# Gated cross-attention block with routed experts: the projection of the first query half is moved from the end of a step to between scores and attend

## The chip, the core and the metric
The kernel runs on one core of a Trainium2 chip. The metric is device time in microseconds (us) of one execution. Three runs of the kernel before gave 631.08, 633.39 and 633.51 us; their median is 633.39 us. A profiled execution of the same kernel gives the rows that are quoted below.

## What is computed
There are 64 sequences of 64 tokens with 128 features, so 4096 tokens. The attention part of the reference, cut to what matters here:

```python
q = (emb @ Wq.T)        # emb = layernorm(x); 16 heads of 64
k = (context @ Wk.T)
v = (context @ Wv.T)
q = _layernorm(q, qn_w, qn_b)
k = _layernorm(k, kn_w, kn_b)
attn = jax.nn.softmax(einsum('bhqd,bhkd->bhqk', q, k) * scale)
out = einsum('bhqk,bhkd->bhqd', attn, v)
x = x + tanh(g) * (out @ Wu.T + bu)
```

After it come a second layer norm, a router that picks 2 of 8 experts for each token, the experts' two-layer networks, a shared expert, and a second gated residual. The change touches the attention part only.

## The kernel before, in words
The tokens are cut into 32 tiles of 128 (two sequences each). A software pipeline runs over steps `s` from -5 to 35. Each engine has its own `step(s)` (ACT from L471, POOL from L645, DVE from L897, PE from L1245), which lists in fixed order what that engine does for several tiles at different stages. The order on each engine is written out by hand, and the engines meet at semaphores. An engine runs its list strictly in order, so an instruction that waits holds up all that stands behind it on that engine.

The tile of a step, in the order of its life:
- `project_qk(n, j, t)` (L1063): the projection of queries (n=0) or keys (n=1), first or second half of the heads (j), as three matmuls of 512 columns (high by high part, low by high, high by low; L1059 to L1061) into PSUM bank `2n+j`. It waits for `n_ready[n][j]`, that is until DVE's `scale` has read what the tile before left in that bank.
- `square` on ACT (L372), `sum_squares` on DVE (L747), a short Newton chain on POOL (L598 to L612), `scale` on DVE (L754): the layer norm of queries and keys.
- `transpose_qk` on PE (L1091), then `transposed` on ACT (L396).
- `project_v` on PE, then `values` on ACT (L404).
- `scores(t)` on PE (L1117): 64 matmuls of 64x64. DVE's `maximum` (L762) and `less_maximum_of` (L769) read them, ACT's `exponential` follows (L411), DVE's `row_sums` (L776) and `row_inverses` (L783), and POOL's `normalise_rows` (L618).
- In the next step `transpose_probabilities` on PE (L1100), `probabilities` on ACT (L418), `attend` on PE (L1132, again 64 matmuls of 64x64), `outputs` on ACT (L426), `project_out` on PE (L1147), `residual` on DVE (L730).
- Later: the second layer norm, `logits` (L1171 on PE, read by `keep_logits`, L794 on DVE), the routing chain on DVE (`route`, L840 to L855, from step 11 on in most steps), and POOL's `scatter` of rows to DRAM (two indirect DMAs a step from step 17 on, L636).

In ACT's step the order around the change is: `probabilities` of tile s-1, `log_variance` and `inverse_root` of the keys, `square(0, 0, s + 2)`, `outputs` of tile s-1 (two), `square(0, 1, s + 2)`, `transposed(0, 0, s + 1)`, `transposed(0, 1, s + 1)`, `exponential(s)`. On DVE, `keep_logits(s - 4)` and `route` stand ahead of the next step's `sum_squares(0, ..)`, `scale(1, 0, ..)`, `row_sums` and `row_inverses`, and then comes `residual`, for which PE's last `transpose_qk` of the step waits. On POOL, `normalise_rows` ends a step and `scatter` begins the next.

Of the kernel before, what the change touches and what calls it, by code (L numbers as in the profile page):

```python
# [41 lines left out]
def flamingo_block(nc, x, xT, ctxT, g_xattn, g_ffn, wqT, wkT, wvT, wuT, bu, qn_w, qn_b, kn_w, kn_b,  # L42
                   wg, w1, b1, w2, b2, ws1, bs1, ws2, bs2, out):

    with ExitStack() as stack:
# [186 lines left out]
        def has(t):  # L232
            return 0 <= t < TILES
# [815 lines left out]
        def _(pe):  # L1049
# [8 lines left out]
            def project(out_bank, t, src, w, j):  # L1058
                nc.tensor.matmul(out_bank, xc_hi[:, t % XD, src, :], w_hi[:, w, cols[j]], start=True, stop=False)  # L1059
                nc.tensor.matmul(out_bank, xc_hi[:, t % XD, src, :], w_lo[:, w, cols[j]], start=False, stop=False)  # L1060
                return nc.tensor.matmul(out_bank, xc_lo[:, t % XD, src, :], w_hi[:, w, cols[j]], start=False, stop=True)  # L1061

            def project_qk(n, j, t):  # L1063
                if has(t):
                    if t == 0:
                        pe.wait_ge(w_ready, (3 if n == 0 else 1) + j)
                    pe.wait_ge(xlo_ready, t + 1)
                    if t >= 1:
                        pe.wait_ge(n_ready[n][j], t)
                    project(ps[2 * n + j][:, :], t, n, n, j).then_inc(proj_done[n][j], 1)  # L1070
# [14 lines left out]
            def transpose_qk(n, j, t, bank_free):  # L1085
                if has(t):
                    bank_free(j, t)
                    pe.wait_ge(n_ready[n][j], t + 1)
                    for a in range(4):
                        c0 = (4 * j + a) * P  # L1090
                        last = nc.tensor.transpose(ps[6 + j][:, a * P:(a + 1) * P], qk_n[:, n, c0:c0 + P], ident[:, :])  # L1091
                    last.then_inc(t_done[n][j], 1)

            def transpose_probabilities(j, t, bank_free):
                if has(t):
                    bank_free(j, t)
                    if j == 0:
                        pe.wait_ge(p_ready, t + 1)
                    for a in range(4):
                        last = nc.tensor.transpose(ps[6 + j][:, a * P:(a + 1) * P],  # L1100
                                                   prob[:, 4 * j + a, :, :].rearrange("p b n -> p (b n)"), ident[:, :])
                    last.then_inc(pt_done[j], 1)

            def scores(t):
                if has(t):
                    for j in range(2):
                        pe.wait_ge(v_ready[j], t + 1)
                    for n in range(2):
                        for j in range(2):
                            pe.wait_ge(T_ready[n][j], t + 1)  # L1110
                    for a in range(PAIRS // 2):
                        for b in range(2):
                            for j in range(2):
                                for h in range(2):
                                    rows = slice(h * HD, (h + 1) * HD)
                                    outs = slice((h ^ j) * HD, ((h ^ j) + 1) * HD)
                                    last = nc.tensor.matmul(ps[4 + j][outs, (2 * a + b) * S:(2 * a + b + 1) * S],  # L1117
                                                            qk_T[rows, 0, 2 * a + j, b * S:(b + 1) * S],
                                                            qk_T[rows, 1, 2 * a + j, b * S:(b + 1) * S], start=True, stop=True)
                    last.then_inc(s_done, 1)  # L1120

            def attend(t):
                if has(t):
                    for j in range(2):
                        pe.wait_ge(pt_ready[j], t + 1)
                    for p in range(PAIRS):
                        at = p % 2 * (PAIRS // 2) + p // 2
                        for h in range(2):
                            for b in range(2):
                                rows = slice(b * S, (b + 1) * S)  # L1130
                                q = (h ^ (p % 2)) * S
                                last = nc.tensor.matmul(ps[6 + b][h * HD:(h + 1) * HD, p * S:(p + 1) * S],  # L1132
                                                        v_sb[rows, t % 2, (2 * p + h) * HD:(2 * p + h + 1) * HD],
                                                        prob_T[rows, at, q:q + S], start=True, stop=True)
                                if p == PAIRS - 1 and h == 1:
                                    last.then_inc(o_done[b], 1)
# [25 lines left out]
            def logits(t):  # L1162
                if has(t):
                    if has(t + 4):
                        pe.wait_ge(sub_ready[1], t + 5)
                    else:
                        pe.wait_ge(lg_ready, t)
                    if t == 0:
                        pe.wait_ge(wg_in, 16)
                    pe.wait_ge(rT_ready, t + 1)  # L1170
                    nc.tensor.matmul(ps[5][:, 0:E], row_T[:, t % 2, :], wg_raw[:, :], start=True, stop=True).then_inc(lg_done, 1)  # L1171
# [10 lines left out]
            def route_ranks(s, lag):  # L1182
                b, at = batch_at(s, lag)
                if b is not None and at == RANKS_AT:
                    ranks(b)

            def transpose_tokens(g):
                pe.wait_ge(norm_ready, GT * g + GT)
                if g == 0:
                    pe.wait_ge(sub_ready[0], TILES)  # L1190
                else:
                    pe.wait_ge(f_lo, g)
                for j in range(GT):
                    last = nc.tensor.transpose(ps[4][:, j * P:(j + 1) * P], rows_all[:, GT * g + j, 0:D], ident[:, :])
                last.then_inc(f_t, 1)

            def shared_hidden(g):
                pe.wait_ge(f_lo, g + 1)
                if g == 0:
                    pe.wait_ge(ffw_ready, len(W1_STEPS))  # L1200
                    pe.wait_ge(w2_in, 3 * 16)
                hi, lo = g_parts[:, g % 2, 0, :], g_parts[:, g % 2, 1, :]
                for c in range(CH):
                    fs = slice(c * P, (c + 1) * P)
                    if g > 0:
                        pe.wait_ge(act_ready, CH * (g - 1) + c + 1)
                    nc.tensor.matmul(ps[c][:, :], w1_hi[:, E, fs], hi, start=True, stop=False)
                    nc.tensor.matmul(ps[c][:, :], w1_hi[:, E, fs], lo, start=False, stop=False)
                    nc.tensor.matmul(ps[c][:, :], w1_lo[:, E, fs], hi, start=False, stop=True).then_inc(h_done, 1)
# [35 lines left out]
            def step(s):  # L1245
                if s == TILES:
                    transpose_tokens(0)
                    transpose_tokens(1)
                    shared_hidden(0)
                transpose_probabilities(0, s - 1, before_p)  # L1250
                transpose_probabilities(1, s - 1, before_p)
                scores(s)
                attend(s - 1)
                project_qk(0, 1, s + 2)
                transpose_qk(0, 0, s + 1, before_q)
                logits(s - 4)
                route_ranks(s, ROUTE_LAG)
                transpose_qk(0, 1, s + 1, before_q)
                project_qk(1, 1, s + 2)
                project_v(0, s + 1)  # L1260
                transpose_normed(s - 3)
                project_out(s - 1)
                transpose_qk(1, 0, s + 1, before_k)
                project_qk(1, 0, s + 2)
                transpose_qk(1, 1, s + 1, before_k)
                project_v(1, s + 1)
                project_qk(0, 0, s + 3)
                if s == TILES:
                    transpose_tokens(2)
                if s == TILES + 1:  # L1270
                    shared_hidden(1)
            steps(step)

            shared_result(0)
# [89 lines left out]
```

## Time and profile before
| what | value |
|---|---|
| three runs | 631.08, 633.39, 633.51 us (median 633.39) |
| span of the profiled execution | 671.8 us (the page gives no other total for it) |
| instructions in the trace | 21158 |
| stretch of the attention steps | about 32 to 414 us of the span |
| matmul instructions | 7642 |

How to read it: the profile is of one execution, and its span of 671.8 us is longer than any of the three runs, so its rows are good for durations, orders and waits, and a sum made of them is a difference against the same span. PE is TensorE's matmuls, PEld its weight loads, DVE VectorE, ACT ScalarE, POOL GpSimd. Matmuls are pipelined: the time from the start of one to the start of the next is what a matmul costs the engine, not its own busy time. An idle time "<-issue" is one in which the engine waited for nothing that the profile shows.

### The profile page before, as it was taken

What the parts mean: (1) busy time and instruction counts of PE and PEld (TensorE: products, weight loads), DVE (VectorE), ACT (ScalarE), POOL (GpSimd) and SP (SyncE); (2) the same over time, 40 slices, a digit from 0 to 9 for tenths busy, and PEclk for the clock granted to TensorE, in tenths of its full rate; (3) what the DMA queues carried; (4) which work ended last, traced back from release to release, by engine and by line L of the source; (5) the groups of instructions that cost most, each with busy time, mean ns of one, the idle gap of its engine ahead of it and who ended that gap; (6) DMA issues with size and microseconds to landing.
All of it is one profiled execution on the core that took longest, in us unless ns stands there. A gap on an engine that the chain in (4) does not pass through costs nothing.

```text
span 671.8 us, 21158 instructions
## 1 busy us (share of the span) xinstructions
PE 586.6 (87%) x7642; PEld 517.3 (77%) x7642; DVE 456.0 (68%) x997; ACT 453.3 (67%) x986; POOL 361.4 (54%) x706
## 2 busy tenths in 40 slices
PE   3889999999999999999999987868979988989930
PEld 1578888888888887877887865766979988989930
DVE  4688889898998888887888874464244534444418
ACT  3688899999897887887887863532525444545425
POOL 2545656565666677677677564554105535545530
PEclk9899999999999999999999999978989989999985
DMA  7900100001001001002000000123102212212228
GB/s 242 282 2 3 34 18 29 24 3 49 4 17 43 26 14 47 25 12 64 11 14 16 10 14 21 34 92 100 41 1 77 76 59 71 73 65 77 73 87 316
DMA packets 22583, 38.01 MB, mean 57 GB/s; under 512 B 5233, under 2 KB 13041, under 8 KB 22353
## 3 DMA queue, kind: packets, MB, share of 16 engines
q1 hardware_dynamic: 17648, 27.27, 12.8%
q0 software_dynamic: 4544, 9.38, 3.9%
q8 instruction: 63, 1.03, 0.7%
q14 instruction: 40, 0.32, 0.2%
q10 hardware_dynamic: 288, 0.00, 0.0%
HBM read 23.17 MB, written 13.47 MB: 55 GB/s over the span
## 4 chain that ended last, share of the span: by engine, by line
PE 74%; DVE 8%; issue 7%; DMA 3%; POOL 2%; ACT 2%; another core or an unknown queue 1%; SPq 0%; ACTq 0%; DVEq 0%; POOLq 0%
PE ps L1317 9%; PE ps L1091 7%; PE ps L1147 7%; PE ps L1059 6%; PE ps L1117 6%; PE ps L1061 5%; PE ps L1060 5%; PE ps L1100 4%; PE ps L1219 4%; PE ps L1132 4%; PE ps L1303 3%; PE ps L1305 3%; PE ps L1304 3%; DMA rows_all<-results 1%; DVE wide L754 1%
## 5 line engine op out<-in xcount | busy, mean ns | idle before, releaser
L670 POOL DMA_INDIRECT results<-spo,xs_ix x78 | 75.2, 965 | 100.9 <-DVE spo L1033 85.9
L522 ACT ACTIVATE qk_T<-ps,b_cols 128x256 f32<-128x256 f32 x156 | 61.8, 475 | 75.7 <-PE ps L1305 74.3
L396 ACT ACTIVATE qk_T<-ps,lnw 128x512 f32<-128x512 f32 x128 | 96.8, 787 | 6.0 <-PE ps L1091 5.4
L1059 PE MATMUL ps<-w_hi,xc_hi 128*128 128x512 f32 x192 | 88.3, 460 | 7.9 <-DVE wide L754 3.7
L754 DVE TENSOR_TENSOR wide<-ps,rstd 128x512 f32<-128x512 f32 x128 | 87.2, 681 | 3.9 <-POOL rstd L612 3.9
L747 DVE TENSOR_REDUCE ss<-wide 128x16 f32<-128x1024 f32 x64 | 77.9, 1218 | 15.5 <-ACT wide L372 13.9
L636 POOL DMA_INDIRECT routed<-rows_all,slot x64 | 64.4, 1006 | 29.9 <-issue 16.0
L1091 PE MATMUL ps<-ident,wide 128*128 128x128 f32 x512 | 78.4, 278 | 2.1 <-DVE wide L754 1.0
L372 ACT ACTIVATE wide<-ps 128x512 f32<-128x512 f32 x128 | 76.1, 596 | 3.2 <-PE ps L1061 3.2
L1061 PE MATMUL ps<-w_hi,xc_lo 128*128 128x512 f32 x192 | 77.2, 402 | 0.0
L1317 PE MATMUL ps<-w_sb,qk_T 128*128 x624 | 76.9, 277 | 0.0
L1060 PE MATMUL ps<-w_lo,xc_hi 128*128 128x512 f32 x192 | 76.5, 398 | 0.0
L1317 PEld LDWEIGHTS ps<-w_sb,qk_T 128*128 128x128 f32 x624 | 73.7, 194 | 0.0
L1091 PEld LDWEIGHTS ps<-ident,wide 128*128 128x128 f32 x512 | 59.2, 145 | 18.3 <-ACT spo L426 7.4
L618 POOL TENSOR_TENSOR prob<-prob,rinv 128x1024 f32<-128x1024 f32 x32 | 61.0, 1907 | 14.9 <-DVE rinv L783 14.7
L762 DVE TENSOR_REDUCE mx<-ps 128x8 f32<-128x512 f32 x64 | 41.2, 686 | 34.5 <-PE ps L1117 34.5
L1147 PE MATMUL ps<-wu_sb,spo 128*128 128x128 f32 x512 | 63.8, 279 | 0.1
L1147 PEld LDWEIGHTS ps<-wu_sb,spo 128*128 128x128 f32 x512 | 61.1, 195 | 3.2 <-issue 0.3
L426 ACT ACTIVATE spo<-ps 128x512 f32<-128x512 f32 x64 | 34.8, 596 | 40.8 <-PE ps L1132 40.8
L1303 PE MATMUL ps<-w_lo,w_hi 128*128 128x256 f32 x156 | 48.7, 312 | 9.4 <-DVE w_lo L1003 9.2
L1117 PE MATMUL ps<-qk_T 64*64 64x64 f32 x2048 | 46.0, 223 | 10.5 <-issue 10.4
L1117 PEld LDWEIGHTS ps<-qk_T 64*64 64x64 f32 x2048 | 37.7, 134 | 20.0 <-issue 19.9
(169 smaller groups left out, 1323.4 us busy)
## 6 DMA issues: line engine op xcount, KB each, us to landing
v_sb<-routed SPq DMA_DIRECT2D x39, 130.0 KB
xc_in<-in_x SPq DMA_DIRECT2D x8, 256.0 KB, 2.9
xc_in<-in_ctx SPq DMA_DIRECT2D x8, 256.0 KB, 4.5
w_raw<-in_L_ffn_W SPq DMA_DIRECT2D x8, 256.0 KB, 2.5
wide<-results SPq DMA_DIRECT2D x4, 512.0 KB, 5.1
rows_all<-results SPq DMA_DIRECT2D x4, 512.0 KB, 8.0
out_x<-x_res SPq DMA_DIRECT2D x8, 256.0 KB, 4.1
x_res<-in_x SPq DMA_DIRECT2D x1, 1792.0 KB, 8.5
```

The costliest lines, as they stand in the source:

```text
L372: nc.scalar.activation(sq[:, n, j * 512:j * 512 + 512], ps[2 * n + j][:, :], ACT.Square, scale=HD ** -0.5).then_inc(sq_ready[n][j], 1)
L396: nc.scalar.activation(qk_T[:, n, 4 * j:4 * j + 4, :].rearrange("p a n -> p (a n)"), ps[6 + j][:, :], ACT.Identity, bias=lnw[:, 2 * n + 1: ...
L670: gp_.indirect_dma_start(out=results[:, :], out_offset=bass.IndirectOffsetOnAxis(ap=xs_ix[:, b4, a:a + 1], axis=0), in_=yb[:, b4, a, :], i ...
L747: nc.vector.tensor_reduce(ss[:, n, :], sq[:, n, :].rearrange("p (h d) -> p h d", h=HEADS), AX.X, ALU.add).then_inc(ss_ready[n], 1)
L754: nc.vector.tensor_tensor(qk_n[:, n, j * 512:(j + 1) * 512].rearrange("p (h d) -> p h d", h=8), ps[2 * n + j][:, :].rearrange("p (h d) -> ...
L1059: nc.tensor.matmul(out_bank, xc_hi[:, t % XD, src, :], w_hi[:, w, cols[j]], start=True, stop=False)
L1060: nc.tensor.matmul(out_bank, xc_hi[:, t % XD, src, :], w_lo[:, w, cols[j]], start=False, stop=False)
L1061: return nc.tensor.matmul(out_bank, xc_lo[:, t % XD, src, :], w_hi[:, w, cols[j]], start=False, stop=True)
L1091: last = nc.tensor.transpose(ps[6 + j][:, a * P:(a + 1) * P], qk_n[:, n, c0:c0 + P], ident[:, :])
L1117: last = nc.tensor.matmul(ps[4 + j][outs, (2 * a + b) * S:(2 * a + b + 1) * S], qk_T[rows, 0, 2 * a + j, b * S:(b + 1) * S], qk_T[rows, 1, ...
L1147: last = nc.tensor.matmul(ps[7][:, 0:D], o_T[:, p, :, :].rearrange("p b n -> p (b n)"), wu_sb[:, p, :], start=(p == 0), stop=(p == PAIRS - 1))
L1317: last_ = nc.tensor.matmul(ps[4 + n % 2][:, a * D:(a + 1) * D], hT[:, n % 2, c, a * P:(a + 1) * P], w2e[:, c, :], start=(c == 0), stop=(c ...
```

## The change
One line of PE's step is moved. Before, the projection of the first query half for tile s+3 was the last of the step (with the next step it is tile s+2 seen from there); after, the projection of the same tile is issued in the next step, between `scores` and `attend`. No other engine's list changes, and no semaphore or buffer is added or removed.

```diff
                 scores(s)
+                project_qk(0, 0, s + 2)
                 attend(s - 1)
                 project_qk(0, 1, s + 2)
...
                 project_v(1, s + 1)
-                project_qk(0, 0, s + 3)
                 if s == TILES:
                     transpose_tokens(2)
```

## Rows read from the trace of the kernel before
**Rows 1.** Page, part 1: busy time, share of the span, instructions.
```profile
PE 586.6 (87%) x7642; PEld 517.3 (77%) x7642; DVE 456.0 (68%) x997; ACT 453.3 (67%) x986; POOL 361.4 (54%) x706
```
**Rows 2.** Busy time by stretch of steps: 1-10, 11-15, 16-29 (us, engines, PEclk, DMA).
```profile
41.57:154.30 112.73, 111.99 (x1882) 98.03 (x1883) 98.47 (x184) 102.44 (x216) 66.46 (x166) 1.00 0.06 17
154.30:212.90 58.60, 56.95 (x955) 49.11 (x954) 52.97 (x112) 52.69 (x113) 34.45 (x86) 1.00 0.09 30
212.90:388.73 175.83, 165.96 (x2653) 140.00 (x2652) 146.12 (x303) 146.67 (x311) 122.80 (x264) 1.00 0.08 24
```
**Rows 3.** Timeline, PE, step 9: start us, busy us, engine, line, operation.
```profile
132.03 1.03 PE L1100 MATMUL ps<-ident,prob 128*128 128x128 f32 x8
132.99 1.16 PE L1117 MATMUL ps<-qk_T 64*64 64x64 f32 x64
133.97 1.11 PE L1132 MATMUL ps<-spo,v_sb 64*64 64x64 f32 x64
135.02 0.50 PE L1059 MATMUL ps<-w_hi,xc_hi 128*128 128x512 f32 x1
...
135.58 0.40 PE L1061 MATMUL ps<-w_hi,xc_lo 128*128 128x512 f32 x1
...
142.48 0.40 PE L1059 MATMUL ps<-w_hi,xc_hi 128*128 128x512 f32 x1
...
143.17 0.49 PE L1100 MATMUL ps<-ident,prob 128*128 128x128 f32 x3
```
**Rows 4.** Timeline, POOL, step 9: the normalisation of the probabilities.
```profile
140.62 1.91 POOL L618 TENSOR_TENSOR prob<-prob,rinv 128x1024 f32<-128x1024 f32 x1
```
**Rows 5.** Timeline, ACT, step 9.
```profile
135.14 1.09 ACT L426 ACTIVATE spo<-ps 128x512 f32<-128x512 f32 x2 [0.47 <-PE ps L1132]
...
137.92 1.08 ACT L411 ACTIVATE prob<-prob 128x1024 f32<-128x1024 f32 x1
```
**Rows 6.** Timeline, DVE, step 9.
```profile
134.22 1.29 DVE L762 TENSOR_REDUCE mx<-ps 128x8 f32<-128x512 f32 x2 [0.29 <-PE ps L1117]
...
139.03 1.22 DVE L776 TENSOR_REDUCE sm<-prob 128x16 f32<-128x1024 f32 x1
```
**Rows 7.** Timeline, PE, step 24.
```profile
313.24 1.06 PE L1100 MATMUL ps<-ident,prob 128*128 128x128 f32 x8
314.23 0.81 PE L1117 MATMUL ps<-qk_T 64*64 64x64 f32 x38
315.35 0.31 PE L1117 MATMUL ps<-qk_T 64*64 64x64 f32 x2 [0.31 <-issue]
316.09 0.57 PE L1117 MATMUL ps<-qk_T 64*64 64x64 f32 x21 [0.43 <-issue]
...
317.65 0.50 PE L1059 MATMUL ps<-w_hi,xc_hi 128*128 128x512 f32 x1
...
318.89 0.29 PE L1171 MATMUL ps<-wg_raw,row_T 128*128 128x8 f32 x2
...
325.84 0.41 PE L1100 MATMUL ps<-ident,prob 128*128 128x128 f32 x2
```
**Rows 8.** Timeline, ACT and DVE, step 24.
```profile
320.51 1.08 ACT L411 ACTIVATE prob<-prob 128x1024 f32<-128x1024 f32 x1
...
319.76 0.16 DVE L794 COPY lg_all<-ps 128x8 f32<-128x8 f32 x1
...
322.22 1.21 DVE L776 TENSOR_REDUCE sm<-prob 128x16 f32<-128x1024 f32 x1
```
**Rows 9.** Timeline, POOL, step 24.
```profile
314.66 0.96 POOL L636 DMA_INDIRECT routed<-rows_all,slot  x1 [0.30 <-issue]
...
323.79 1.91 POOL L618 TENSOR_TENSOR prob<-prob,rinv 128x1024 f32<-128x1024 f32 x1 [0.30 <-DVE rinv L783]
```
**Rows 10.** Timeline, PE, two attends with a gap (steps 4 and 15).
```profile
78.51 0.56 PE L1132 MATMUL ps<-spo,v_sb 64*64 64x64 f32 x19 [0.61 <-issue]
204.25 0.39 PE L1132 MATMUL ps<-spo,v_sb 64*64 64x64 f32 x10 [0.74 <-issue]
```

## The prediction
> **What bounds the kernel now.** I read the page first. PE has the most busy time, 87% of the span, and DVE, ACT and POOL follow at 54 to 68% [rows 1]. A share over the whole span doesn't say whether PE has room in the steps that the change touches, so I cut those steps into three stretches: steps 1 to 10, before the routing chain runs on DVE; steps 11 to 15, with routing; and steps 16 to 29, which nearly all have POOL's scatters too [rows 2]. They take 112.73, 58.60 and 175.83 us, which is 11.27, 11.72 and 12.56 us a step. In the first PE is busy for 111.99 of 112.73 us; in the last for 165.96 of 175.83, so there it does wait.
>
> Then I read one step on all engines, from one L1100 to the next. Step 9 takes 143.17 - 132.03 = 11.14 us [rows 3]. Two loops run through it. The first is PE's own work, back to back, 11.14 us. The second is the way from a tile's attend to the next probabilities: attend, ACT's two outputs (L426), which end the idle time of ACT, then with ACT never idle up to the exponential (L411, 137.92 to 139.00) [rows 5], DVE's row sums (L776, start 139.03, 0.03 us behind the exponential) [rows 6], and POOL's normalisation (140.62 + 1.91 = 142.53) [rows 4]. In step 24 PE starts L1100 0.14 us after POOL's end (323.79 + 1.91 = 325.70, L1100 at 325.84) [rows 7, 9]. So the second loop closes in 142.53 - 132.03 + 0.14 = 10.64 us. It has 0.50 us to spare in step 9, and none in step 24, which takes 12.60 us.
>
> Step 24 is longer mostly since the scores stand still twice, with 38 of 64 matmuls done (315.35 and 316.09, both "issue") [rows 7]. Its row sums don't wait for the exponential: that ends at 321.59, they start at 322.22, behind the routing chain on DVE [rows 8]. So the exponential has 0.63 us to spare there.
>
> **The change, part by part.** It adds and removes no instruction. Three matmuls of 512 columns, with their wait for DVE's `scale`, leave the place behind `project_v` and come to stand between scores and attend. No DMA and no other engine's queue is touched. The wait itself costs nothing: in the order of DVE that `scale` lies ahead of the sums for the scores that PE has just finished, in the step before. Behind the waiting projection on PE stand attend and all the rest.
>
> (1) What PE saves at the end of a step: three matmuls from 142.48 to L1100 at 143.17, 0.69 us or 0.23 each [rows 3]. In step 9 this only makes PE reach L1100 earlier, where it will wait for POOL.
>
> (2) What it costs in its new place. No row shows a 512-column matmul between two groups of 64x64 ones. The nearest is attend followed by a projection [rows 3]: 64 small matmuls that another small group follows take 133.97 - 132.99 = 0.98 us, and 64 that a projection follows take 135.02 - 133.97 = 1.05, so leaving small tiles costs 0.07. The first two matmuls of the projection take 135.58 - 135.02 = 0.56 us, not 0.46, and the third 0.23. That is 0.86. Entering small tiles again costs something too: from eight transposes to the scores is 0.96 us, about 0.09 more than eight of their spacing (0.109 us, my estimate from the same timeline). Sum **0.95 us** later for attend. The ends are 0.69 (the price at the end of a step) and 1.05; I take 0.95 because it is from the nearest rows.
> The Trainium skill (TensorE: Matmul & The Clock Gate, Back-to-back issue gap) gives 518 cycles for a 512-column matmul, at any place, by which three would cost 0.65 us; the row says 0.56 for two alone behind small tiles. By the page the whole change would come out near no change, which is the first rival.
>
> (3) Steps 1 to 10. Attend 0.95 us later moves outputs, the two transposes, their copies and the exponential by 0.95, since ACT goes through them without a pause; the loop becomes 10.64 + 0.95 = 11.59 us. PE's own loop becomes 11.14 - 0.69 + 0.95 = 11.40, so the bound passes from PE to this loop. Ten steps: 115.9 against 112.73, **+3.2 us**. This counts a gain already: two attends of all steps have a large "issue" gap (0.61 and 0.74 us idle) [rows 10], and some have small ones, in which the instructions came late. A projection between the two bursts of small matmuls gives them up to 0.95 us more to arrive, so I let such gaps vanish (about 3 us over all stretches, estimated from the start times of the small matmuls in seven attends).
> The Trainium skill (Runtime: NRT & Kernel Launch, Instruction fetch mechanics) says the cost of crossing an instruction block is mostly hidden. If that held for all these gaps, nothing would be relieved, and the sum would be about 3 us higher.
>
> (4) Steps 11 to 15. The row sums wait for DVE, not for the exponential. DVE pays another way: its statistics end a step's tail, whose squares now come some 0.5 us later against L1100, and its idle time before the maxima was 0.29 us [rows 6]. I put 0.26 us a step on the routing ones, less where a gap vanishes: **+0.7 us**.
>
> (5) Steps 16 to 29. Attend is fed slower there after a stall; with a projection ahead of it the instructions can pile up, so I take 0.10 off: 0.85 us later. The exponential takes 0.85 - 0.63 = 0.22 of it into the loop. The logits come 0.85 later too: L1171 ends at 319.18, L794 starts at 319.76 [rows 7, 8], 0.58 to spare, so 0.27 goes into DVE's chain. The larger counts: 12.60 + 0.27 = 12.87, for 14 steps 180.2 against 175.83, **+4.4 us**. The stall in the scores stays: it lies ahead of the projection, beside POOL's scatters (314.66 [rows 9]).
>
> (6) The first step loses the cover too, +0.4, bounded by 0 and 0.95. Steps 30 and on have no such projection and nothing changes; nor does the expert part, 260 us.
>
> Sum: 3.2 + 0.7 + 4.4 + 0.4 = 8.7 us, on a span of 671.8. The profiled execution is 38 us longer than the median run, so I carry over the difference alone: 633.39 + 8.7, about **642.0 us**. If the stalls in the scores belong to the profiled execution, the last stretch behaves like the first, at 0.45 less the same slack, and the sum hardly moves.
>
> **The rivals.**
> No change: if the projection costs only 0.69 us between small tiles, the loop in steps 1 to 10 is 11.33, ten of them +0.6; the late steps swallow it within 0.58 and 0.63 us, except the two without routing (some 0.2 each, +0.4); with +0.3 for steps 11 to 15 and +0.4 at the start the sum is +1.7, 635.1 us. For it: PE is idle for 10 us of the last stretch. Against it: the 0.56 us.
> Faster: the instruction stream is what falls short in the scores, and the projection gives it time. If both gaps in the late scores went, starts at 316.09 in place of some 314.9, the 14 steps would fall by 1.2 - 0.27 = 0.93 each, -13 us, with +4.3 elsewhere -8.7 us, 624.7. It decides at whether the gaps lie behind the projection; with 38 of 64 matmuls done they lie ahead of it, and only a shift of the whole order against POOL would move them.
> Worse than forecast: the gaps in attend stay (+3), the entry into small tiles costs more, and square(0, 0), now ready later, holds up outputs on ACT; ACT was idle for 0.47 us there [rows 5], so up to 0.3 us a step in ten steps, +3. Together 648.
>
> **How the numbers follow.** A measurement tells about 0.5% (3.2 us) from no change. My forecast, with its own spread of 638 to 646, has 0.62; worse 0.12; no change 0.18; faster 0.08. For slower by over 0.5% that makes 0.74, with 0.18 within 0.5% and 0.08 faster. The range takes in the bounds of the unknown costs and reaches to the second case: 634.5 to 647.5, leaving out the faster case and the far end of the worse one.
>
> **What would show it.** In the changed profile: attend's first matmul 0.95 us after the last score matmul; steps 1 to 10 of 11.6 us with PE idle before L1100, released by POOL; the exponential 0.95 us later against L1100; steps 16 to 29 near 12.9 us with the scores' two gaps unchanged; attends without gaps. I am wrong if steps 1 to 10 stay at 11.2 us, or if the scores' gaps shrink.

## The result and the profile after

The changed kernel takes **645.0 us** (median of four runs, 644.14 to 646.89) against 633.45 us for the kernel before (four runs, 631.08 to 634.48). The ratio is 1.0199, with a 95% interval of 1.0175 to 1.0223. That is 11.6 us slower, where 8.7 were forecast; 645.0 lies inside the range, which ended at 647.5.

The profile of before that the prediction reads is of an execution of 671.8 us, 38 us above the median run. Single executions are like that, and on one of the chips used all of them were (662 to 671 us for the kernel before), so the stretches below are compared with a second profile of the unchanged kernel (first experiment, span 629.4 us), and each experiment with the kernel before on its own chip.

Page, part 1, of the changed kernel (span 645.1 us, its own time 646.89):

```profile
PE 583.2 (90%) x7642; PEld 508.7 (79%) x7642; DVE 458.3 (71%) x997; ACT 451.3 (70%) x986; POOL 360.6 (56%) x706
```

The counts of instructions are those of [rows 1]. PE is still the busiest. As before, that share doesn't say what bounds a step. Next comes the view by stretch (columns as in [rows 2]; rows are steps 1 to 10, 11 to 15, 16 to 29, and the rest). First a repeated profile of the changed kernel (span 640.3 us, the last of three), which had the fewest gaps:

```profile
41.63:159.97 118.34, 116.56 (x1883) 96.68 (x1883) 99.00 (x184) 102.32 (x216) 66.29 (x166) 1.00 0.05 16
159.97:219.56 59.59, 58.59 (x955) 48.91 (x955) 53.10 (x112) 52.31 (x114) 34.05 (x85) 1.00 0.09 29
219.56:385.59 166.03, 163.69 (x2655) 136.59 (x2656) 147.16 (x302) 145.34 (x311) 122.59 (x264) 1.00 0.08 25
385.59:640.30 254.71, 215.69 (x2003) 206.67 (x2003) 131.78 (x361) 126.22 (x300) 119.84 (x132) 0.95 0.25 84
```

And the unchanged kernel, second profile:

```profile
42.14:154.71 112.57, 111.89 (x1883) 98.03 (x1884) 98.54 (x184) 102.47 (x217) 66.38 (x166) 1.00 0.05 17
154.71:212.52 57.81, 56.93 (x956) 49.11 (x954) 52.87 (x112) 52.70 (x114) 34.48 (x86) 1.00 0.10 30
212.52:374.56 162.04, 159.41 (x2653) 137.42 (x2652) 146.53 (x303) 146.51 (x311) 122.87 (x264) 1.00 0.09 26
374.56:629.40 254.84, 215.73 (x2003) 206.57 (x2003) 131.17 (x361) 125.94 (x300) 119.93 (x132) 0.95 0.25 84
```

The differences are +5.8, +1.8, +4.0 and -0.1 us, 11.5 in all, against the measured 11.6. That they meet so closely is in part luck: the profile of the run at 646.89 us has +5.5, +2.6, +4.9 and +1.3. In both nearly the whole loss lies in steps 1 to 29; what follows them moves by -0.1 and +1.3.

One step on all engines shows how. Timeline of PE, step 9 of the changed kernel (start us, busy us, engine, line, operation; it answers to [rows 3]):

```profile
138.11 1.07 PE L1100 MATMUL ps<-ident,prob 128*128 128x128 f32 x8
139.10 1.16 PE L1117 MATMUL ps<-qk_T 64*64 64x64 f32 x64
140.20 0.50 PE L1059 MATMUL ps<-w_hi,xc_hi 128*128 128x512 f32 x1
140.54 0.40 PE L1060 MATMUL ps<-w_lo,xc_hi 128*128 128x512 f32 x1
140.78 0.40 PE L1061 MATMUL ps<-w_hi,xc_lo 128*128 128x512 f32 x1
141.10 1.16 PE L1132 MATMUL ps<-spo,v_sb 64*64 64x64 f32 x64
142.19 0.50 PE L1059 MATMUL ps<-w_hi,xc_hi 128*128 128x512 f32 x1
...
149.39 0.40 PE L1061 MATMUL ps<-w_hi,xc_lo 128*128 128x512 f32 x1
149.84 0.63 PE L1100 MATMUL ps<-ident,prob 128*128 128x128 f32 x4
```

The step takes 149.84 - 138.11 = **11.73 us** in place of 11.14. From scores to attend are 2.00 us (141.10 - 139.10), where [rows 3] have 0.98: attend starts 1.02 later. It then takes 1.09 itself and not 1.05, so what reads it comes 1.06 to 1.08 later. The last matmul of the last projection begins at 149.39, and the next instruction could follow 0.23 later; L1100 comes 0.45 later. PE waits.

What it waits for is in the timelines of ACT, DVE and POOL in the same step (these answer to [rows 4 to 6]). ACT:

```profile
142.31 1.09 ACT L426 ACTIVATE spo<-ps 128x512 f32<-128x512 f32 x2 [0.51 <-PE ps L1132]
...
145.09 1.08 ACT L411 ACTIVATE prob<-prob 128x1024 f32<-128x1024 f32 x1
```

DVE:

```profile
146.20 1.22 DVE L776 TENSOR_REDUCE sm<-prob 128x16 f32<-128x1024 f32 x1 [0.41 <-ACT prob L411]
```

POOL:

```profile
147.79 1.90 POOL L618 TENSOR_TENSOR prob<-prob,rinv 128x1024 f32<-128x1024 f32 x1
```

Counted from L1100, L426 starts at 4.20 (before 3.11), the exponential at 6.98 (5.89), and POOL ends at 11.58 (10.50). Every one is 1.08 to 1.09 later. PE starts 0.15 behind POOL's end. The chain that was 10.64 us long is now 11.73, and it has passed PE.

The waits of PE over the attention steps (who waits, for whom, us in total, times, longest; short ones like that of step 9 are not in the list) point the same way. Changed kernel:

```profile
PE ps L1100 <- POOL prob L618: 4.0, 14, 0.9
```

Unchanged kernel, second profile:
```profile
PE ps L1100 <- POOL prob L618: 1.3, 3, 0.5
```

In steps with routing another row decides. ACT, step 12, changed kernel (L1100 at 173.56, the next at 185.44: 11.88 us):

```profile
180.53 1.08 ACT L411 ACTIVATE prob<-prob 128x1024 f32<-128x1024 f32 x1
```

DVE, the same step:

```profile
179.23 0.17 DVE L794 COPY lg_all<-ps 128x8 f32<-128x8 f32 x1 [0.37 <-PE ps L1171]
...
181.81 1.21 DVE L776 TENSOR_REDUCE sm<-prob 128x16 f32<-128x1024 f32 x1
```

DVE, step 12 in the second profile of the unchanged kernel (L1100 at 166.22 and 177.67: 11.45 us):

```profile
171.45 0.15 DVE L794 COPY lg_all<-ps 128x8 f32<-128x8 f32 x1
...
174.05 1.21 DVE L776 TENSOR_REDUCE sm<-prob 128x16 f32<-128x1024 f32 x1
```

The copy of the logits starts 5.67 us after L1100 in place of 5.23, and now waits for PE; the routing chain behind it keeps its length, so the row sums start at 8.25 in place of 7.83, and the step is 0.43 longer. The exponential has ended 0.20 us before the row sums start. It is the logits that set this step, by 1.02 less a slack of about 0.6.

### The profile page after: what moved, and what is told of

Its sections match the earlier page's. It is cut to its first block, busy times and chain, and to the rows that moved or that the text cites. A ratio compares the mean times of both kernels' runs of the same rounds, so it can differ in the third digit from the quotient of the medians.

```text
span 645.1 us, 21158 instructions
## 1 busy us (share of the span) xinstructions
PE 583.2 (90%) x7642; PEld 508.7 (79%) x7642; DVE 458.3 (71%) x997; ACT 451.3 (70%) x986; POOL 360.6 (56%) x706
## 4 chain that ended last, share of the span: by engine, by line
PE 70%; DVE 8%; POOL 7%; issue 6%; ACT 5%; DMA 2%; POOLq 0%; DVEq 0%; ACTq 0%; SPq 0%
PE ps L1317 10%; PE ps L1059 6%; PE ps L1132 5%; PE ps L1117 5%; PE ps L1091 5%; PE ps L1100 5%; PE ps L1147 5%; POOL prob L618 5%; PE ps L1061 4%; PE ps L1060 4%; PE ps L1219 4%; PE ps L1303 4%; PE ps L1304 3%; PE ps L1305 3%; DVE sm L776 2%
## 5 line engine op out<-in xcount | busy, mean ns | idle before, releaser
L1059 PE MATMUL ps<-w_hi,xc_hi 128*128 128x512 f32 x192 | 92.0, 479 | 6.7 <-DVE wide L754 3.2
L1091 PEld LDWEIGHTS ps<-ident,wide 128*128 128x128 f32 x512 | 61.1, 146 | 14.1 <-ACT spo L426 7.7
L426 ACT ACTIVATE spo<-ps 128x512 f32<-128x512 f32 x64 | 34.8, 596 | 21.4 <-PE ps L1132 21.4
L1059 PEld LDWEIGHTS ps<-w_hi,xc_hi 128*128 128x128 f32 x192 | 37.0, 193 | 15.9 <-DVE w_lo L690 5.5
L1003 DVE TENSOR_TENSOR w_lo<-ps,w_lo 128x256 fp32r<-128x256 f32 x39 | 16.5, 424 | 44.4 <-ACT w_lo L513 44.4
```

## The experiments

The theory was the forecast's: attend comes later, and the chain attend, outputs, exponential, row sums, normalisation, transposes takes the bound from PE. The rivals were that PE's own extra work is the loss, and, for the gaps in the small matmuls, that they come from POOL's scatters or from the supply of instructions.

### 1. The unchanged kernel again
No edit.

> The kernel before, unchanged, for a second profile. Its first profiled execution had a span of 671.8 us, 38 us over the median of its runs, and stood still for 1.2 us in the scores of most steps from 16 on; the changed kernel's profile has none of that. Theory A: those gaps belong to that one execution; the new profile has a span near 632 us, steps 1 to 10 of 11.15 us and steps 16 to 29 of some 11.5 us without gaps in the scores. Theory B: the gaps belong to the order of the kernel before, and the change takes them away; then they are here again and the span is near 670.

Measured: 630.99 us (628.38 to 634.25, ten runs), ratio 0.9991 (0.9969 to 1.0012), span 629.4. No step has a gap in the scores, though the scatters stand where they stood. What remains are six gaps in attend, 4.1 us in all: steps 4 (0.63), 6 (0.49), 15 (0.48), 24 (0.66), 26 (1.22) and 28 (0.66), each from the start of one small matmul to the start of the next. One more pause, of 0.5 us, stands in step 13 directly behind the last matmul of attend. The base of term (5) of the prediction, a late step of 12.6 us, was that of the profiled execution. The same steps take 11.3 to 11.5 us here where they have no gap.

### 2 and 3. The end of the chain made shorter, without and with the change
POOL's normalisation treats 8 of its 16 groups. The other half of the probabilities stays unnormalised.

```diff
-nc.gpsimd.tensor_tensor(pv, pv, rinv[:, :]...to_broadcast([P, 2 * PAIRS, S]), ALU.mult)
+nc.gpsimd.tensor_tensor(pv[:, 0:PAIRS, :], pv[:, 0:PAIRS, :], rinv[:, 0:PAIRS]...to_broadcast([P, PAIRS, S]), ALU.mult)
```

> The kernel before, with POOL's normalisation of the probabilities over the first 8 of 16 groups of columns only (half the work is left out, so its 1.91 us become about 1). That shortens the way from scores and attend to the next probabilities by some 0.9 us and touches PE not at all. Theory 1 (two bounds: PE's own work of 11.15 us a step, and this way): steps 1 to 10 stay at 11.15, only steps with routing, where the way is longer, fall to 11.2; in all 2 to 5 us faster than before, about 630. Theory 2 (the way is the bound everywhere): 0.9 us in each of 29 steps, over 20 us faster.

> The changed kernel with the same half of the normalisation left out. Theory 1: the way from attend to the probabilities no longer bounds it, and what is left over the shortened kernel before is PE's own extra work, a projection between two groups of 64x64 matmuls at 1.03 us in place of 0.69 at the end of a step: steps of 11.5 us, about 0.35 us in each of 30 steps or 10 us over the shortened kernel before, about 640. Rival (the whole loss is attend coming later, PE's work is unchanged): steps of 11.15 us, both shortened kernels the same, about 630.

Measured: without the change 625.63 us (ratio 0.9909, 0.9885 to 0.9933), with it 634.4 (1.0039, 1.002 to 1.0059). PE, step 9 without the change, from one L1100 to the next:

```profile
132.01 1.04 PE L1100 MATMUL ps<-ident,prob 128*128 128x128 f32 x8
...
143.19 0.38 PE L1100 MATMUL ps<-ident,prob 128*128 128x128 f32 x2
```

PE, step 9 with the change:

```profile
132.95 1.04 PE L1100 MATMUL ps<-ident,prob 128*128 128x128 f32 x8
...
144.41 0.38 PE L1100 MATMUL ps<-ident,prob 128*128 128x128 f32 x2
```

POOL in the same step, its normalisation at 1.04 us in place of 1.90:

```profile
142.60 1.04 POOL L618 TENSOR_TENSOR prob<-prob,rinv 128x512 f32<-128x512 f32 x1
```

Without the change the step stays at 11.18 us: shortening POOL gives nothing in steps 1 to 10, because the chain had room there. With the change it falls from 11.73 to 11.46. POOL ends at 143.64, 0.77 us ahead of L1100, so PE is the bound again. This splits the 0.59 us a step: **0.3 are PE's own extra work, and 0.27 more are the chain.** Both totals missed their forecasts from the same side. Without the change 2 to 5 us were expected and 6.6 came (632.26 to 625.63), in the profiles mostly in steps 16 to 29 (158.9 us for 162.0, a step 29 of 10.7 for 11.4 among them). The forecast of some 640 us for the changed kernel stood on that base of 630: its 10 us of extra over the shortened kernel before were near the measured 8.8, and its step of 11.5 us came. In steps 1 to 10 the shorter normalisation takes 0.27 us off each, and in the routing steps 0.4 (11.88 to 11.47, PE's own time again). Between 2 and 3 the change still costs 8.8 us (634.4 - 625.63) in the medians and 4.9 in the spans of the two profiles (631.8 - 626.9). Ten times 0.3 us is the part that steps 1 to 10 show. In experiment 2 most routing steps still take 11.27 to 11.51 us, with PE waiting for DVE's `residual`, so there the difference is smaller. The medians differ by more than the profiles because of the executions that were profiled: that of 2 was the slowest of its six (628.68 us, with pauses of 1.10 and 0.99 us in two attends), that of 3 the second fastest of nine (633.53). What the faster executions of 2 save isn't on record.

### 4. The projection ahead of the scores
```diff
+                project_qk(0, 0, s + 2)
                 scores(s)
                 attend(s - 1)
...
-                project_qk(0, 0, s + 3)
```

> The projection of the first query half ahead of the scores, behind the transposes of the probabilities, so that scores and attend are adjacent as before and no extra change between 64x64 and full tiles is made. Theory 1: PE's own work is 11.15 to 11.25 us again, but both scores and attend come 0.7 to 0.8 us later after the probabilities are ready: steps 1 to 10 take 11.4 us (11.72 in the changed kernel), steps with routing, whose way runs through the scores and DVE, some 12.1 (11.87); in all about as slow as the changed kernel, 642 to 646. Rival (the extra change of tile size is the whole cost): steps as before, about 634.

Measured: 643.77 us (1.0204, 1.017 to 1.0237). PE, step 9:

```profile
134.26 1.06 PE L1100 MATMUL ps<-ident,prob 128*128 128x128 f32 x8
...
135.95 1.16 PE L1117 MATMUL ps<-qk_T 64*64 64x64 f32 x64
136.93 1.11 PE L1132 MATMUL ps<-spo,v_sb 64*64 64x64 f32 x64
...
145.63 0.41 PE L1100 MATMUL ps<-ident,prob 128*128 128x128 f32 x2
```

Scores and attend are 0.98 apart, as in [rows 3], and attend starts 2.67 us after L1100 against 1.94: 0.73 later. The chain gives 10.64 + 0.73 = 11.37, and the step takes 145.63 - 134.26 = 11.37. Here the small matmuls stay together, so nothing is paid for a second change of tile size. The total is the same as with the change, since the scores are late too: the steps with routing take 11.98 to 12.23 us.

### 5. Both query halves between scores and attend
```diff
                 scores(s)
+                project_qk(0, 0, s + 2)
+                project_qk(0, 1, s + 2)
                 attend(s - 1)
-                project_qk(0, 1, s + 2)
...
-                project_qk(0, 0, s + 3)
```

> Both query halves are projected between scores and attend; the second no longer stands between attend and the first transposes. Theory 1 (what stands between scores and attend passes into the step one to one, and the change between 64x64 and full tiles is paid once, by the first projection): attend's first matmul 1.03 + 0.69 = 1.72 us after the last score matmul, steps of 11.72 + 0.69 = 12.4 us, routing or not, some 14 us over the changed kernel, 658 to 661. Rival (the second projection is for nothing, as PE is waiting for POOL at the end of a step anyway): steps stay at 11.7 to 11.9, 645 to 648.

Measured: 699.52 us on a chip where the kernel before takes 665.95 (1.0497, 1.0432 to 1.0562). The absolute number of the expectation doesn't apply there; the length of the early steps does. PE, step 9, and then the scores of a late step:

```profile
141.77 1.06 PE L1100 MATMUL ps<-ident,prob 128*128 128x128 f32 x8
142.76 1.16 PE L1117 MATMUL ps<-qk_T 64*64 64x64 f32 x64
...
145.46 1.16 PE L1132 MATMUL ps<-spo,v_sb 64*64 64x64 f32 x64
...
154.19 0.41 PE L1100 MATMUL ps<-ident,prob 128*128 128x128 f32 x2
...
341.85 0.31 PE L1117 MATMUL ps<-qk_T 64*64 64x64 f32 x2 [0.25 <-issue]
342.58 0.63 PE L1117 MATMUL ps<-qk_T 64*64 64x64 f32 x24 [0.42 <-issue]
```

Scores to attend are 2.70 us, 1.72 more than before and 0.70 more than with the change. The step is 12.42 us, 0.69 more than 11.73. PE does the same work in both kernels and needs only 11.46 us for it by experiment 3, so this 0.69 is attend's lateness, and it passes on one to one. The gaps in the late scores are there too, at the same 38 of 64 matmuls as in [rows 7]. "12.4 us, routing or not" missed: steps 16 to 29 take 13.77 us on the mean, and the loss over the kernel before is 33.6 us where 26 to 29 were implied (658 to 661 against 632). Against the profile of experiment 7, which has the order of the kernel before on the same chip, the steps are longer by 1.16 us in 1 to 10 (124.20 for 112.56 us) and by 1.28 in 16 to 29 (192.76 for 174.85). So gaps in the scores neither cover a late attend nor shrink by it.

### 6. Projection ahead of the scores, with the shorter normalisation
The edits of 2 and 4 together; half of the probabilities stays unnormalised.

> The projection ahead of the scores, with half of POOL's normalisation left out, so that PE's own work is the bound. Theory 1 (the 0.3 us that PE has more to do in the changed kernel are the extra change between 64x64 and full tiles): steps 1 to 10 at 11.18 us, as with the short normalisation in the kernel before (11.17), against 11.47 in the changed kernel; steps with routing up to 11.4; in all near 626 to 628. Rival (any move away from the end of the step costs PE the 0.3 us): steps of 11.47, about 634.

Measured, on the same chip as 5: 651.53 us (0.9778, 0.9726 to 0.9829). Steps 3 to 10 take 11.15 to 11.17 us, but for step 4, which has a pause in attend. With the chain out of the way in both, the 0.3 us to 3 (11.46) is what the place between scores and attend costs PE alone: leaving small tiles once more and entering them again.

The total is 14.4 us under the kernel before, where the expectation implied 4 to 6. Most of the surplus is in steps 16 to 29, 164.6 us against 174.9 in the profile of 7: most of their scores stand still once, shortly, and not twice. Step 24, PE:

```profile
306.42 0.80 PE L1117 MATMUL ps<-qk_T 64*64 64x64 f32 x37
307.40 0.64 PE L1117 MATMUL ps<-qk_T 64*64 64x64 f32 x26 [0.18 <-issue]
```

POOL, its second scatter:

```profile
306.00 0.96 POOL L636 DMA_INDIRECT routed<-rows_all,slot  x1 [0.30 <-issue]
```

The scores start 1.67 us after L1100 here (0.99 in [rows 7]) and the scatters no later, yet the gap still comes after 37 matmuls, when the second scatter is over. Whether the place of the projection or the shorter normalisation shortens it was not separated.

### 7 and 9. Shifting PE's instructions
Idle 64x64 matmuls go to PE at the very start, where it waits for the weights, 64 and then 32 of them. Their float32 form takes two matmul instructions and two weight loads each, so PE's program is 256 and 128 instructions longer.

```diff
             pe.wait_ge(centre_ready, 1)
+            for _ in range(64):   # 32 in the second kernel
+                nc.tensor.matmul(ps[7][0:HD, 0:S], ident[0:HD, 0:HD], ident[0:HD, 0:S], start=True, stop=True)
```

> The kernel before, with 64 idle 64x64 matmuls (128 instructions) issued on PE while it waits for the first weights. In the profiles of the kernel before and of the changed one every gap of more than 0.2 us in attend lies at a PE instruction whose count is 191 modulo 256, in steps 4, 6, 15, 24, 26 and 28. Theory A (the instruction stream comes in blocks of 256, and a block is late when its boundary falls late in the dense stretch): with 128 instructions more the gaps leave those steps and come in others, at the same count modulo 256: candidates are 5 (matmul 41), 7 (31), 14 (59), 16 (41), 25 (50), 27 (40); the total stays at 2 to 5 us and the time within 2 us of the kernel before. Theory B (the gaps belong to those steps, through other traffic in them): the gaps stay in steps 4, 6, 15, 24, 26 and 28.

> In the run before, 64 idle fp32 matmuls turned out to be 128 matmul instructions with as many weight loads, so 256 instructions: a whole block, and the gaps in attend stayed at the same count modulo 256 and in steps 2, 4, 6 and 15. Now 32 idle matmuls, which is 128 instructions, half a block. Theory A (blocks of 256 instructions): no gap over 0.2 us in steps 2, 4, 6, 15, 24, 26 and 28; those that come have the count 191 or 192 modulo 256 and lie in other steps, candidates 5 (matmul 41), 7 (31), 14 (59), 16 (41), 25 (50), 27 (40). Theory B: they stay in steps 4, 6 and 15.

Measured: 674.54 us against 665.95 for the first (1.0109, 1.0045 to 1.0174), 633.92 against 632.6 for the second (1.0022, 1.0005 to 1.004). With 256 more, the gaps over 0.2 us stay in steps 2, 4, 6 and 15 (24, 26 and 28 have none, as in the first profile of before, which also has the gaps in the scores). With 128 more they leave those, and stand in steps 1 (0.85), 3 (0.92), 5 (0.50), 14 (0.79), 16 (1.27) and 29 (1.07); three of the six candidates named (5, 14, 16) are among them. Steps 3 and 4 of the second kernel on PE (L1134 is attend there):

```profile
68.41 0.46 PE L1134 MATMUL ps<-spo,v_sb 64*64 64x64 f32 x16 [0.70 <-issue]
...
78.77 1.11 PE L1134 MATMUL ps<-spo,v_sb 64*64 64x64 f32 x64
```

Counting loads, matmuls and semaphore instructions of PE from the first, every such gap in the attends of steps 1 to 31 in 1, 7 and 9, and in the profile after (steps 6, 15, 24, 26), stands at 191 or 192 modulo 256. So these gaps belong to a place in the instruction stream, not to data or to POOL. Not every such place costs time. In the second profile of before 32 of them fall into the scores or the attend of steps 1 to 31. The 16 in the scores pass without a pause, and so do nine in attend; the seven pauses all come at the 34th matmul of attend or later. The first of the two kernels was meant to move the gaps and couldn't, as its 256 are a whole period. That it is 8.6 us slower lies at its start: the idle matmuls outlast the wait for the weights.

```profile
2.31 13.88 PE L1053 MATMUL ps<-ident 64*64 64x64 f32 x128 [2.31 <-POOL centre L550]
```

The first matmul on the weights starts at 16.12 us there and at 7.88 in the first profile of before, and step 1 at 49.84 for 41.59. The 32 of the second kernel end at 9.4 us, and its step 1 starts at 41.95.

### 10 and 11. Room for the chain from the routing
If DVE's routing holds up the row sums, it may stand elsewhere. These edits are on the kernel before: DVE's routing chain goes behind `row_inverses` of the next step, or ahead of its maxima. ACT's two exponentials of the router move with it, behind the copies of the probabilities in 10 and ahead of `outputs` in 11. (The routing chain runs from L810 to L855, so L811 below is one of its operations.) DVE's part of the edits:

```diff
+                route(s - 1, ROUTE_LAG)   # 10: behind row_inverses; 11: behind second_statistics
...
-                route(s, ROUTE_LAG)
```

> The kernel before, with the routing chain on DVE moved behind the row sums and row inverses of the next step (and ACT's two exponentials of the router behind the copies of the probabilities). In the steps with routing (17 of 29) the row sums wait for DVE, which still works at the chain, and the step takes 11.27 to 11.52 us in place of 11.15. Theory: with the chain out of the way these steps fall to 11.15 to 11.3, 2 to 5 us in all, about 629 on a chip where the kernel before takes 632. Rival (DVE has no room anywhere, the chain only moves the wait to the second sum of squares and on to PE): same time as before.

> The kernel before, with the routing chain in another place than in the run before: there its second operation stood still for 1.95 us beside POOL's normalisation (L811, 0.23 us in the kernel before), ahead of the residual for which PE waits, and the steps took 13.1 us. Now the chain stands behind the statistics and ahead of the maxima, where DVE waits for the scores and POOL's normalisation is over; ACT's two exponentials of the router stand ahead of its wait for attend. Theory: maxima 0.3 to 0.6 us later, which the way from the scores has to spare in the kernel before (0.50 us), so the 17 steps fall from 11.27 to 11.52 to 11.15 to 11.3 us, 2 to 5 us faster. Rival (the way from the scores has nothing to spare once DVE is later): same time, or up to 2 us slower.

Measured: 658.07 us (1.0401, 1.0377 to 1.0426) and 636.22 (1.0074, 1.0049 to 1.0098). The theory and the rival missed in both: 25 us slower, and 4 us where at most 2 were allowed for. DVE in 10, a routing step:

```profile
164.39 1.95 DVE L811 TENSOR_TENSOR w_raw<-lg_all,w_raw 128x64 f32<-128x64 f32 x1
166.63 0.35 DVE L730 SCALAR_TENSOR_TENSOR x_res<-ps,tg,x_res 128x128 f32<-128x128 f32 x1
```

POOL at the same time:

```profile
164.36 1.90 POOL L618 TENSOR_TENSOR prob<-prob,rinv 128x1024 f32<-128x1024 f32 x1
```

An operation on 128x64 elements, 0.22 us long in the kernel before, takes 1.95 when POOL's normalisation has started 0.03 us ahead of it, and ends 0.08 us behind it. Each of the first four parts of the chain has one operation that grows to 1.95 us like this. `residual` and a `scale` stand behind it, and PE waits for those: most routing steps take 13.0 to 13.2 us. The Trainium skill (SBUF — State Buffer, SBUF: two separate sides) says that a VectorE operation with two SBUF inputs and a GpSimd operation that reads SBUF exclude each other for a whole instruction; these rows agree. In 11 the slots for the scatter come a step later, and POOL, which waits for them, holds up its variance chain; DVE then waits for it (step 16):

```profile
220.07 0.69 DVE L754 TENSOR_TENSOR wide<-ps,rstd 128x512 f32<-128x512 f32 x1 [2.51 <-POOL rstd L612]
```

Steps 16 and 24 take 13.7 to 13.9 us, and most routing steps 11.50 to 11.58. The place of the routing in the kernel before is better than both. No kernel tried that computes the whole result was faster than the kernel before.

### 8 and 12. The changed kernel again
No edit to it.

> The changed kernel, unchanged, again. The kernel before took 632 us on one chip and 666 us on another, where the scores stand still twice in every step from 16 on while POOL starts its scatters. Here is the question what the change does on the chip of this call. Theory: the loss is the way from scores to the next probabilities (0.58 us in steps 1 to 10) and has nothing to do with those gaps: 11 to 13 us over the kernel before on a chip of the first kind, 8 to 13 us on one of the second, and there the gaps of 1.2 us stay in the scores, ahead of the projection. Rival: on a chip of the second kind the projection takes the gaps away or covers them, and the change is no loss there.

> The changed kernel once more, on whatever chip this call has. On two chips on which the kernel before took 632 us the loss was 11 to 12 us. If this is a chip on which it takes some 666 us (gaps in the scores from step 16 on): theory, a loss of 8 to 13 us too, gaps unchanged; rival, the gaps shrink and the loss with them. If it is one of the first kind: 11 to 13 us again.

Measured: 643.91 us (1.0179, 1.015 to 1.0208) and 645.24 (1.0223, 1.0195 to 1.0251). In three measurements the change costs 1.8 to 2.2%. Steps 1 to 10 take 11.71 to 11.74 us in both, but for those with a gap (step 4 and 6 in the second, 12.25 and 12.30; step 6 in the third, 12.84). The late scores have no gaps in either, so the rival wasn't put to the test. The gaps in attend vary between executions. The sum of those gaps is 2.5 us in the profile after, 1.7 in the second and 1.04 in the third, where step 6 alone has one:

```profile
103.22 0.79 PE L1132 MATMUL ps<-spo,v_sb 64*64 64x64 f32 x35
104.83 0.69 PE L1132 MATMUL ps<-spo,v_sb 64*64 64x64 f32 x29 [0.83 <-issue]
```

## Why the prediction was right, and which terms it mis-sized

The mechanism held, and the time came inside the range: attend comes later, the chain behind it was 0.50 us from the bound, and it becomes the bound. The sum was 8.7 us where 11.6 came. By its own steps, against the second profile of before and the third of after:

| step of the prediction | forecast | measured |
|---|---|---|
| (1) PE saves at the end of a step | 0.69 | 0.69; PE arrives early and waits for POOL |
| (2) attend later | 0.95 | 1.02 at its start, 1.08 at its end |
| (3) steps 1 to 10 | +3.2 | +5.8 |
| (4) steps 11 to 15 | +0.7 | +1.8 |
| (5) steps 16 to 29 | +4.4 | +4.0 |
| (6) first step | +0.4 | 0 |

**Step (2) is the mis-sized term.** Its parts were 0.07 for leaving small tiles, 0.56 and 0.23 for three matmuls, 0.09 for entering them. The rows have 1.10 against 0.98 from the scores to the projection, so 0.12 for leaving; 0.58; and 0.32 for the third matmul with the entry: 1.02. It left out that attend behind a projection is itself slower (1.09 against 1.05). With those 1.08 the prediction's own sum for the chain, 10.64 + 1.08, gives 11.72 for the measured 11.73.

**Step (3)** was 2.6 us short, and three parts make it up. The chain's 0.14 us a step is 1.4 us. The assumption that the gaps in attend vanish is 1.04: one gap stayed. The remaining 0.16 is the difference between the two profiles of before. The assumption that all gaps go was not met: the gap stands at a fixed place in the instruction stream, and with one projection ahead of attend some remain. Over all steps the gaps in attend fell from 4.1 us to between 1.0 and 2.5, where the forecast counted about 3 us of relief. But the first profile of before has only 2.6, so how much of the fall is the projection's doing and how much is the spread between executions isn't shown. With two projections ahead of attend (5) none is left in steps 1 to 31, in one profile. The Trainium skill (Runtime: NRT & Kernel Launch, Instruction fetch mechanics) speaks of blocks of 256 instructions, which is the period found in 7 and 9, and says that crossing one is mostly hidden. By count that holds here, for 25 of 32 places in small matmuls; late in attend it cost 0.2 to 1.3 us.

**Step (4)** named the wrong tail. It charged 0.26 us for DVE's statistics; the rows of step 12 show the logits, 0.44 later, and the step 0.43 longer. That is the mechanism of step (5), a delay less 0.58 of slack, which belonged in steps 11 to 15 as well: 5 x 0.43 = 2.2; steps 13 and 15, whose pauses vanished, lost only 0.20 each, which leaves the 1.8.

**Step (5)** came out near by two errors that cancel. The delay wasn't 0.85 but 1.02 and more, so that a routing step lost 0.43 and not 0.27; without the gaps the 14 steps lost about 6.5 us (4.0 + 2.54 of gaps that the third profile of after doesn't have). The 0.10 taken off for instructions that pile up isn't seen: in steps 1 to 10 and later, scores to attend are 1.98 to 2.07 us alike. The base of 12.6 us was the profiled execution's own, and the sum set 14 times step 24 (176.4 us) against a stretch of 175.83: by its own 0.27 a step it should have been 3.8. The prediction had covered this by its sentence that the last stretch then behaves like the first, and for the sign that was right. The changed kernel was never run where late scores have gaps, so whether it would alter them was not measured. With both halves between (5) they stayed; with the projection ahead of the scores and the shorter normalisation (6) they shrank.

**Step (6)** was nothing. From the first scores (L1117 at 32.57 and 32.06 in the two profiles) to L1100 of step 1 are 9.57 us in both: in the second profile of before PE could have gone on 0.4 us before L1100 and waited for POOL, and no attend stands behind the projection in the step ahead of it.

Of the rivals, no change needed 0.69 us between the small groups; 1.02 was measured. The three matmuls alone take 0.90 there (141.10 - 140.20), so the 0.65 that the prediction quotes for them at any place was not met in this one. Faster needed a shift of the gaps in the scores; in ten of the fourteen profiles there are none. Worse, at 648, was right about two of its parts, the gaps that stay and the dearer entry, and the result lies between it and the forecast. Its third part, `square(0, 0)` holding up ACT, did not happen: ACT waits 0.51 us for attend ahead of L426, more than its 0.47 before.

## What to carry to other kernels

Ask of a moved piece of work not only what its engine saves and pays, but what stands behind it and how much room the longest chain through that has. Here an engine that was 99% busy had a chain 0.50 us behind it, so any delay of attend over that was lost in full (0.73 us in experiment 4 cost 0.23 a step), and filling the end of PE's step could give nothing back. Price a small piece between two groups of another tile size by the rows on both sides of it, entry and exit, and count the first instructions behind it too.

## What the runs showed of the hardware

- Going from 64x64 tiles to full ones and back costs PE about 0.3 us: three matmuls of 512 columns take 0.69 us among their like and 1.02 between two groups of small ones.
- In attend, a run of 64x64 matmuls that follows another with nothing or little between, PE can stand still for 0.2 to 1.3 us at one place in every 256 of its instructions, from the 29th matmul on; in most attends it doesn't. Shifting the program by 128 instructions moved all these gaps; their sum was 5.4 us for 4.1.
- The first profile of before (671.8 us) differs from the second in two places. The late scores stand still twice, as in [rows 7], and what follows step 29 takes 283 us and not 255 (276 to 277 in 5, 6 and 7). The cause of both is open.
- A small DVE operation can last 1.95 us for 0.22 beside one of POOL's, and the trace shows it as busy, not as waiting.

That the scatters alone don't make the gaps in the scores is seen in the profile after, which has none. Its step 24, PE:

```profile
317.98 1.16 PE L1117 MATMUL ps<-qk_T 64*64 64x64 f32 x64
```

POOL over the same scores:

```profile
317.01 1.10 POOL L636 DMA_INDIRECT routed<-rows_all,slot  x1 [0.17 <-issue]
318.41 0.96 POOL L636 DMA_INDIRECT routed<-rows_all,slot  x1 [0.31 <-issue]
```
